# Attention kernel for 16 images: two batches in one turn of the loop over the middle batches

## The reference

```python
qkv = jnp.einsum('bchw,oc->bohw', x, w_qkv)
q, k, v = jnp.split(qkv, 3, axis=1)            # 8 heads of 64
q = q.reshape(b, HEADS, HEAD_DIM, n) * SCALE
sim = jnp.einsum('bhdi,bhdj->bhij', q, k)
attn = jax.nn.softmax(sim, axis=-1)
out = jnp.einsum('bhij,bhdj->bhid', attn, v)
y = jnp.einsum('bchw,oc->bohw', out, w_out) + b_out[None, :, None, None]
mean_sq = jnp.mean(y * y, axis=1, keepdims=True)
y = y * jax.lax.rsqrt(mean_sq + SCALE) * rms_scale[None, :, None, None]
return y + x
```

## Time and profile before

| | us |
|---|---|
| timed runs | 4695.69, 4701.51, 4702.99 |
| median | 4701.51 |
| the profiled execution, its own time | 4695.66 |
| its span, first to last instruction | 4693.9 |
| PE busy in it | 4245.9 (90%) |
| DVE, POOL, ACT busy | 3011.2, 2728.8, 2270.9 |

### The profile page before, as it was taken

How to read it: one execution, slowest core, us unless ns; L and a number is a source line. 1 busy time by engine, 2 the same in 40 slices (tenths; PEclk the granted TensorE clock), 3 DMA queues, 4 the chain that set the end, 5 groups by cost and what they waited for, 6 DMA issues and landing times.

```text
span 4693.9 us, 64715 instructions
## 1 busy us (share of the span) xinstructions
PE 4245.9 (90%) x18624; PEld 2462.7 (52%) x18624; DVE 3011.2 (64%) x2651; ACT 2270.9 (48%) x3969; POOL 2728.8 (58%) x2077
## 2 busy tenths in 40 slices
PE   7998989989899898998989899899998999989996
PEld 4555555555555555555555555555555555555552
DVE  4666666666756666666666666666657666576665
ACT  3444454454444444544454454544545445454453
POOL 4556556556555665656656555665556655566555
PEclk9999999999999999999999999999999999999997
DMA  3011110110111101101011010111111111111010
GB/s 127 36 46 46 37 57 34 46 50 32 63 38 37 63 19 64 41 33 63 19 64 45 33 59 20 63 45 37 55 39 43 46 37 54 46 37 46 37 36 27
DMA packets 71387, 213.53 MB, mean 45 GB/s; under 512 B 8152, under 2 KB 8280, under 8 KB 58208
## 3 DMA queue, kind: packets, MB, share of 16 engines
q1 hardware_dynamic: 71008, 208.80, 12.4%
HBM read 168.92 MB, written 39.85 MB: 44 GB/s over the span
## 4 chain that ended last, share of the span: by engine, by line
PE 66%; DVE 21%; issue 11%; ACT 1%; POOL 0%; DVEq 0%; DMA 0%; ACTq 0%; POOLq 0%; SPq 0%
PE aux L423 16%; PE pv L539 16%; DVE maxima L772 12%; PE aux L455 8%; PE aux L479 7%; PE aux L511 6%; PE score L524 5%; PE score L526 4%; DVE inv_sum L812 3%; DVE y_sb L832 3%; PE pv L498 2%; DVE k_l L766 1%; DVE x_lo L271 1%; PE aux L487 1%; ACT probs L613 0%
## 5 line engine op out<-in xcount | busy, mean ns | idle before, releaser
L916 POOL TENSOR_TENSOR prob_sum<-prob_sum,probs 128x512 f32<-128x512 f32 x1536 | 2005.4, 1329 | 903.3 <-ACT probs L613 902.7
L772 DVE TENSOR_REDUCE maxima<-aux 128x1 fp32r<-128x1024 f32 x1024 | 1200.2, 1213 | 1080.7 <-PE aux L511 1079.3
L613 ACT ACTIVATE probs<-score 128x512 f32<-128x512 f32 x2048 | 1113.8, 594 | 1013.3 <-PE score L526 980.3
L539 PE MATMUL pv<-probs,v_sb 128*64 128x512 f32 x4096 | 1011.6, 615 | 0.0
L524 PE MATMUL score<-q_hl,k_hh 128*128 128x512 f32 x2048 | 907.4, 443 | 84.4 <-ACT probs L613 49.3
L912 POOL TENSOR_TENSOR prob_sum<-probs 128x512 f32<-128x512 f32 x256 | 338.1, 1343 | 909.3 <-ACT probs L613 909.3
L526 PE MATMUL score<-q_hm,k_l 72*128 72x512 f32 x2048 | 825.2, 403 | 0.0
L423 PE MATMUL aux<-x_hi,w_ring 128*128 128x512 f32 x2048 | 683.6, 416 | 83.2 <-DVE maxima L772 65.9
L524 PEld LDWEIGHTS score<-q_hl,k_hh 128*128 128x128 f32 x2048 | 390.5, 191 | 425.7 <-issue 223.7
L539 PEld LDWEIGHTS pv<-probs,v_sb 128*64 128x64 f32 x4096 | 252.2, 138 | 493.1 <-issue 424.6
L423 PEld LDWEIGHTS aux<-x_hi,w_ring 128*128 128x128 f32 x2048 | 371.2, 195 | 248.0 <-DVE maxima L772 141.6
(11 more groups left out here) (61 smaller groups left out, 4179.5 us busy)
## 6 DMA issues: line engine op xcount, KB each, us to landing
w_ring<-w_split SPq DMA_DIRECT2D x93, 1024.0 KB, 4.9
x_stage<-x SPq DMA_DIRECT2D x128, 256.0 KB, 4.1
resid<-x SPq DMA_DIRECT2D x128, 256.0 KB, 6.3
out<-resid SPq DMA_DIRECT2D x128, 256.0 KB, 2.0
w_split<-w_ring SPq DMA_DIRECT2D x3, 1024.0 KB, 12.5
w_split<-y_sb SPq DMA_DIRECT2D x3, 1024.0 KB, 3.8
y_sb<-wqkv SPq DMA_DIRECT2D x4, 512.0 KB, 8.2
probs<-wqkv SPq DMA_DIRECT2D x2, 512.0 KB, 7.2
```

The source lines that it names most:

```text
L539: pe.matmul(pv[half][e * D:(e + 1) * D, :], v_sb[:, pair // 2, j, (pair % 2) * P + e * D:(pair % 2) * P + (e + 1) * D], probs[:, j % 4, e, ...
L613: act.activation(probs[:, j % 4, e, :], score[e][:], ACT.Exp, scale=SOFT).then_inc(prob_ready, 1)
L772: dve.tensor_reduce(maxima[:, n:n + 1], bank(k, 2), AX_X, ALU.max).then_inc(aux_free[k], 1)
L916: pool.tensor_tensor(prob_sum[:, e, :], prob_sum[:, e, :], probs[:, j % 4, e, :], ALU.add).then_inc(prob_added, 1)
```

## The change

The loop's step becomes 2, and each turn holds the code of two batches, b and b + 1, one behind the other. It now has 7 turns. The batches, their order and every operation in them stay the same.

```diff
@@ -120,6 +120,7 @@
     LOOPS = B - 2
+    assert LOOPS % 2 == 0
     bodyz = AuxCounts(body_items(False, True), [s + LOOPS * n for s, n in zip(loop.start, per_batch)])
@@ -281,8 +282,9 @@
             one(Body(body0, 0, True, False))
-            with eng.Fori(1, 1 + LOOPS) as b:
+            with eng.Fori(1, LOOPS, 2) as b:
                 one(Body(loop, b, False, False))
+                one(Body(loop, b + 1, False, False))
             one(Body(bodyz, B - 1, False, True))
```

## The result

| | before | changed |
|---|---|---|
| median, us | 4702.25 (4695.65 to 4706.80, 6 runs) | 4678.35 (4673.28 to 4678.98, 6 runs) |
| profiled execution, us | 4695.66 | 4678.98 |
| its span, us | 4693.9 | 4676.2 |

The ratio is 0.995, with a 95% interval of 0.9937 to 0.9963. So the changed kernel is faster by 24 us, 0.5%, where 29 were forecast. The two profiled executions differ by 16.7 us only (their spans by 17.7).

What follows compares the result with a forecast made beforehand. TensorE, busy 90% of the span, was taken as the bound. Seven back edges at 4.2 us gave 29.4 us, other terms 0: 4666.3 us from the profiled run, 4672.1 from the median, forecast 4669, range 4659 to 4681.

Steps and rivals of the forecast that it cites:

- Step (1): Loop end, all engines: seven taken branches go, 4.2 us each, 29.4 us gained, at least 25.9, at most 32.9.
- high end: Back edge price of 4.7 us: 13 turns of 290.13 us against the turn without a jump, 285.4.
- low end: Back edge price of 3.7 us: slot 7 to slot 3, 154.5 us across a taken branch, 150.8 across the last.
- The path: Behind a taken branch, first exponentials lose 3.1 us, ACT resuming after PE; a further 0.9 comes from PE's lower clock.
- Step (2): Second batch's waits and addresses from b + 1: no added register operations per batch, costed at 0, with 0 to 1 us.
- Step (3): Six back edges kept with a longer body: 0 change, plus or minus 1 us each, 6 us in all.
- sign of being wrong: At inner seams: the forecast is wrong if slots 1 to 3 give back more than 0.5 us of the gain.
- Step (4): DVE and SP may newly stop at the six edges; DVE's 3.2 us lies under 6.5 us of cover; costed at 0.
- "slower" rival: Body too long for DVE, its stop outlasting its cover before the maxima reduce: 17 us slower, 4713 us; chance 0.02.
- seam rival: Loss belongs to the seam between batches, not the branch: time stays at 4696 to 4702 us; chance 0.03.
- branch-alone rival: Only the branch instruction goes, 45 ns on ACT, seven being 0.3 us: 4695.4 us, no change; chance 0.02.
- The level: Whole-kernel time: 4666.3 us from the profiled run or 4672.1 from the timed median; which would show was left open.

Runs made afterwards that it cites:

- E1: Against the kernel before, only PE and ACT do two batches per turn, the other engines one; median 4678.23 us, ratio 0.9949.
- E3: Against the kernel before, only ACT does two batches per turn, the other engines one; median 4701.74 us, ratio 1.0000.
- E2: Against the kernel before, only PE does two batches per turn, the other engines one; median 4678.08 us, ratio 0.9953.
- E12: Against the kernel before, only PE's order ending slot 7 changes: first half of Q, T, V3, second half of Q; median 4710.65 us, ratio 1.0018.
- E8: Against the kernel before, the fourteen middle batches are written out without a loop on all engines, counts being constants; median 4631.57 us, ratio 0.9851.
- E4: Against the kernel before, only DVE, POOL and SP do two batches per turn, PE and ACT one; median 4703.31 us, ratio 1.0003.
- E6: Against the kernel before, all engines do seven batches per turn, two turns with one taken branch; median 4656.08 us, ratio 0.9908.
- E5: Against the kernel before, only PE's order ending slot 7 changes: V3 first, then T, then all of Q; median 4656.40 us, ratio 0.9903.

## Why the prediction was right, and where it was not

- *The direction and the range* held: 4678.35 lies in 4659 to 4681. It lies near the upper end, as the gain was 24 and not 29 us.
- *Step (1), the price of a back edge*, was mis-sized. I put 4.2 us, with 3.7 and 4.7 as ends; the steady turns of the changed kernel show 3.5, below my low end. Seven of those are 24.4 us; the first turn took 0.6 us more in the profile after, the six jumps 0.4 in all, and 23.4 are left. Both ends compared seams that differ in something else. The high end took the loop's first turn, of 285.4 us, for one like the inner ones, and those take 286.6. Why a first turn is shorter is open: it differs in slots 1 and 2, and the time at the lower clock does not explain it, as the first turns of E1 and E3 took 286.0 us with 17.1 us of it and that of the kernel before 285.4 with the same 17.1. The low end took the last batch, which has constants: from slot 7 to slot 3 it was 150.8 us, an inner seam 151.1.
- *The path* was wrong in two points. I read the 3.1 us by which the first exponentials were late as lost, with ACT's stop ending last. E2 and E3 show ACT's stop to be free in this kernel, and the loss to be PE's. And I put the rest down to the clock; E12 had the clock up and PE's L511 no earlier, held by a second stop that my account did not have. The sum was not touched, as it went by whole seams.
- *Step (2)*, no added register work, held for the change: the inner seam's batch does not take longer than the one that jumps. But that register operations cost little in general, which I carried into E8, was wrong.
- *Step (3)*: the six remaining edges kept their price but for 0.07 us each, batches of 290.1 to 290.3 us and PE's stop at 3516 ns in the median. Slots 1 to 3 of the inner seams' batches gave back 0.4 us, just under the 0.5 that I had named as a sign of being wrong.
- *Step (4)*: VectorE's stop went from 0.4 to 2.8 us and was covered; E4 has it alone, with no loss in the loop part. The "slower" rival thus had its mechanism but not its price. That the stop appears as the turn grows from 342 to 680 instructions agrees with the rule of the Trainium skill cited there ("Runtime: NRT & Kernel Launch", section "Instruction fetch mechanics"); POOL, which stops at 366, still does not.
- *The seam rival and the branch-alone rival* are both ruled out by the result and by E6: 12 jumps fewer, 41 us, at seams that otherwise remained.
- *The level*: I could not tell which level the median would show; it showed the higher one, 4678, as the median of before did, 4702. That the levels are early and late starts fits the profiles (5.5 us of start and 0.6 of the first turn, against 5.9), but only profiled runs show their start.

## What to carry to other kernels

In this kernel the loop's back edge cost what the bounding engine's stream lost; ACT's stop ended later and cost nothing. Look for the stop in the loop's own line, then ask what is queued ahead of it, and look some microseconds further for a second one. If the stop can't be removed, try ending the turn on that engine with its longest instructions; here this was worth more than doing two batches per turn, while half of it (E12) lost. And try writing the loop out on the bounding engine alone, since each engine can have its own.

## What the runs showed of the hardware

- A taken branch to the head of a long turn stops a sequencer for 3.4 to 3.9 us on PE (2388 instructions) and 3.1 to 3.5 on ACT in the kernel before; a turn of 342 instructions on DVE made it 0.3, one of 680 made it 2.8 to 3.1.
- Behind such a jump PE's stream stopped a second time: its M group started 2.3 to 2.6 us behind the next 16 KB packet of its instruction queue at all 13 jumps of the kernel before and all 13 of E12, whether the granted clock had been up or not.
- After 1.6 to 2.2 us of idle time at a seam PE's granted clock fell to the lower level for 3.4 us, at all 13 jumps of the kernel before; after 0.33 to 0.87 us (E5) it stayed up at all 13, after 0.96 to 1.44 us (E12) at 12 of 13.
- ACT's stop is no fixed time: 3.1 to 3.5 us in the kernel before, 3.6 to 4.1 in E5, 4.5 to 6.0 in E12, where only PE's order at the seam differs.
- Register operations: dropping them with the jumps gained 1.7 us a batch over the kernels without a jump when all engines did (286.6 to 284.9) and 3.4 when PE alone did (283.3); on the other four alone, with their jumps, nothing.
- Batches came in a few lengths, 283.3, 285.0, 286.6, 290.1 and 293.4 us; small differences of delay at a seam did not reach the batch's length.
